# Looked-up ids broadcast by DMA as 16-bit halves, and empty GpSimd instructions between early gathers, in a recommendation tower on one core

## The reference, cut to what matters

```
e = stack([tbl_f[ids[:, f]] for f in 39 fields], axis=1)     # (512, 39, 32) float32
z = einsum('bpc,apc,bpa->bp', e[:, ROW], w, e[:, COL])       # 741 pairs (i<j) of fields
h = relu(concat([z, dense_ctx], 1) @ W_top1 + b_top1)        # 757 -> 512
h = relu(h @ W_top2 + b_top2)                                # 512 -> 256
y = h @ W_top3                                               # (512, 1)
```

## Time and profile before

| | |
|---|---|
| median of 3 runs | 199.92 us (199.55 to 202.13) |
| the profiled execution: its time | 198.71 us |
| its span | 197.0 us |
| granted TensorE clock | 1.00 of full |
| busy: TensorE, VectorE, GpSimd, ScalarE | 184.5, 144.1, 135.4, 42.7 us |

### The profile page before, as it was taken

One profiled execution on the slowest core, in us unless ns is written; L12 is line 12 of the kernel. 1 busy time (PEld: TensorE's weight loads), 2 busy tenths in 40 slices (PEclk: granted clock), 3 DMA queues, 4 the chain that ended last, 5 costly groups with the idle time before them and its releaser, 6 DMA issues.

```text
span 197.0 us, 3278 instructions
## 1 busy us (share of the span) xinstructions
PE 184.5 (94%) x1320; PEld 64.4 (33%) x1320; DVE 144.1 (73%) x137; ACT 42.7 (22%) x64; POOL 135.4 (69%) x202
## 2 busy tenths in 40 slices
PE   6999988969999999999999999799989976999895
PEld 3534533332222222322322222223322212222782
DVE  4889998965899989976663999589664349747600
ACT  4956941030001100111112100110121111210722
POOL 7988899888888888888888888888922200440000
PEclk9999999999999999999999999999999999999999
DMA  6999940000000100000000000000000000000000
GB/s 166 278 290 419 387 138 15 10 17 12 10 13 10 20 10 12 12 14 13 10 13 14 11 13 10 15 13 15 12 0 3 0 0 0 0 5 0 0 0 0
DMA packets 6688, 9.75 MB, mean 49 GB/s; under 512 B 1977, under 2 KB 4477, under 8 KB 6673
## 3 DMA queue, kind: packets, MB, share of 16 engines
q1 hardware_dynamic: 3696, 8.00, 12.6%
q0 software_dynamic: 2944, 1.51, 4.4%
q10 hardware_dynamic: 32, 0.03, 0.1%
HBM read 9.53 MB, written 0.00 MB: 48 GB/s over the span
## 4 chain that ended last, share of the span: by engine, by line
POOL 55%; PE 32%; issue 7%; DVE 2%; DMA 1%; ACT 1%; DVEq 0%; POOLq 0%
POOL gathered L395 41%; POOL pause L402 13%; PE ps L609 10%; PE ps L623 10%; PE ps L634 6%; PE ps L654 4%; PE ps L646 2%; DVE prod L518 2%; DMA gathered<-tbl,ids_sb 1%; POOL sel L384 1%; PE ps L587 1%; PE ps L663 0%; ACT eT L448 0%; POOL sel L387 0%; ACT z_sb L455 0%
## 5 line engine op out<-in xcount | busy, mean ns | idle before, releaser
L518 DVE TENSOR_TENSOR prod<-ps,eT 128x1024 f32<-128x1024 f32 (+2 forms) x91 | 110.2, 1265 | 36.2 <-PE ps L609 31.6
L395 POOL DMA_INDIRECT gathered<-tbl,ids_sb x92 | 92.3, 1003 | 15.2 <-issue 15.0
L609 PE MATMUL ps<-eT,w_sb 32*128 32x512 f32 (+2 forms) x380 | 70.7, 640 | 4.4 <-DVE prod L518 2.9
L623 PE MATMUL ps<-prod,sel 128*32 128x512 f32 x380 | 51.5, 604 | 0.0
L609 PEld LDWEIGHTS ps<-eT,w_sb 32*128 32x128 f32 (+2 forms) x380 | 22.0, 183 | 52.0 <-issue 25.1
L402 POOL MEMSET pause<- 128x256 f32 x91 | 30.3, 333 | 0.1
L503 DVE TENSOR_SCALAR hot<-ids_half,row_of 125x2048 bf16<-125x2048 f16 x34 | 27.8, 881 | 1.5 <-PE ps L576 0.9
L409 POOL TENSOR_TENSOR tabs<-tabs 128x512 f32<-128x512 f32 x8 | 10.1, 1264 | 25.0 <-ACT tabs L469 25.0
L576 PE MATMUL ps<-hot,lower 125*32 125x512 bf16 x272 | 22.0, 401 | 0.0
L634 PE MATMUL ps<-z_sb,w_sb 128*128 128x512 f32 x40 | 20.4, 624 | 0.7 <-ACT eT L448 0.7
L623 PEld LDWEIGHTS ps<-prod,sel 128*32 128x32 f32 x380 | 8.1, 108 | 33.7 <-issue 21.0
(11 more groups left out here) (36 smaller groups left out, 63.5 us busy)
## 6 DMA issues: line engine op xcount, KB each, us to landing
w_sb<-w SPq DMA_DIRECT2D x1, 1536.0 KB
gathered<-tbl,ids_sb POOLq DMA_INDIRECT x92, 2.3
tabs<-hot SPq DMA_DIRECT2D x3, 448.0 KB
w_sb<-wst SPq DMA_DIRECT2D x1, 640.0 KB, 13.1
w_sb<-wst SPq DMA_DIRECT2D x1, 576.0 KB, 12.0
tabs<-hot SPq DMA_DIRECT2D x1, 560.0 KB
w_sb<-wst SPq DMA_DIRECT2D x1, 512.0 KB, 10.5
w_sb<-w SPq DMA_DIRECT2D x1, 512.0 KB
```

The costliest lines, as they stand in the source:

```text
L395: pool.indirect_dma_start(gathered[J][:, b, K * r:K * r + K], None, tables[f], bass.IndirectOffsetOnAxis(ap=ids_sb[:, F * b + f:F * b + f ...
L518: dve.tensor_tensor(prod[:, x:x + n, :], ps[:, s:s + n, :], eT[:, I:I + 1, :].broadcast_to([P, n, B]), ALU.mult).then_inc(multiplied, 1)
L609: mm = pe.matmul(ps[:, RUN_BANK[p] + i - first, :], w_sb[rows, w_tile(q), :], eT[rows, J, :], start=True, stop=True)
L623: mm = pe.matmul(z_ps[K * (u % G):K * (u % G) + K, :], sel[:, u // G, :], prod[:, RUN_SLOT[p] + t - FIRST_TILE[p], :], start=(u < G), stop ...
```

## The change

The ids of the looked-up fields are laid out as 16-bit halves (the low half of each id) in one row of 2,048 for each h. Four loads, each of one such row to 125 partitions, take the place of the load, the conversion, the spreading matmuls and the copies. The load for h = 0 is on ScalarE's queue, the other three on SyncE's, each ahead of table h. `ids_half` is uint16 where it was float16. The "lower" step of h = 0 is cut into two halves of four slices, and "lower" 3 now stands behind "keep" 1 and before "keep" 2 on ScalarE. Look-up 2 has PSUM banks of its own (4, 5). Fourteen bf16 matmuls of 128 x 512 on zeros stand ahead of TensorE's work.

On GpSimd only the row numbers are made before the gathers. The five steps that make `ident` and `sel` follow gathers 1 to 5, one each. Between gathers 6 to 20 and their successors stand two `engine_nop`, each followed by a wait for its own semaphore. From gather 21 on there is the clear of `pause` as before.

```diff
-WARM = [2, 2]
+BARE = 20
+WARM = 14
+LOWER_PIECES = [[(0, 4), (4, 8)], [(0, 8)], [(0, 8)], [(0, 10)]]
...
-    steps += [("ids", 0), ("lower", 0), ("ids", 1), ("hot", 0, 0, 8), ("look", 0, 0, 3), ("lower", 1), ("ids", 2),
-              ("look", 0, 3, 8), ("keep", 0), ("lower", 2), ("ids", 3), ("hot", 1, 0, 8), ("look", 1, 0, 8),
-              ("lower", 3), ("keep", 1), ("hot", 2, 0, 8), ("look", 2, 0, 8), ("keep", 2), ("hot", 3, 0, 4),
+    steps += [("lower", 0), ("hot", 0, 0, 8), ("look", 0, 0, 8), ("lower", 1), ("keep", 0), ("hot", 1, 0, 8),
+              ("look", 1, 0, 8), ("lower", 2), ("keep", 1), ("hot", 2, 0, 8), ("look", 2, 0, 8), ("lower", 3),
+              ("keep", 2), ("hot", 3, 0, 4),
...
-        ids_half = [sb(f"ids_half{h}", [P, G, B], F16) for h in range(NHOT)]
+        ids_half = [sb(f"ids_half{h}", [P, G, B], U16) for h in range(NHOT)]
...
+            def load_hot_ids(h):
+                sp.dma_start(ids_half[h][0:HP, :, :].rearrange("p f b -> p (f b)"),
+                             hot_ids[h:h + 1, :].broadcast_to([HP, G * B])).then_inc(hot_ids_in[h], 16)
+
             sp.dma_start(ids_sb[:, :], ids).then_inc(ids_in, 16)
             load_table(0)
+            load_hot_ids(1)
             load_table(1)
+            load_hot_ids(2)
             load_table(2)
+            load_hot_ids(3)
...
+                    gathers += 1
+                    if gathers == 1:
+                        pool.memset(ident[:, :], 0.0).then_inc(consts_zero, 1)
+                    elif gathers == 2:
+                        pool.wait_ge(consts_zero, 1)
+                        pool.affine_select(out=ident[:, :], in_=ident[:, :], compare_op=ALU.not_equal, fill=1.0,
...
+                    elif gathers <= BARE:
+                        for _ in range(2):
+                            pool.engine_nop().then_inc(passed, 1)
+                            passes += 1
+                            pool.wait_ge(passed, passes)
+                    elif gathers < NCHUNK * len(fields):
+                        if pauses:
+                            pool.wait_ge(paused, pauses)
                         pool.memset(pause[:, :], 0.0).then_inc(paused, 1)
...
-            act.dma_start(hot_ids_sb[:, :], hot_ids).then_inc(hot_ids_in, 16)
-            act.wait_ge(hot_ids_in, 16)
-            act.activation(ids16[:, :], hot_ids_sb[:, :], ACT.Copy).then_inc(ids16_made, 1)
+            act.dma_start(ids_half[0][0:HP, :, :].rearrange("p f b -> p (f b)"),
+                          hot_ids[0:1, :].broadcast_to([HP, G * B])).then_inc(hot_ids_in[0], 16)
...
+            zeros = prod[:, 0, :].bitcast(BF16)
+            for _ in range(WARM):
+                pe.matmul(ps[:, 7, :], zeros[:, 0:P], zeros[:, 0:B], start=True, stop=True)
```

More of the change, by code:

```diff
@@ L207, in turns, with lowers_of @@
     return TURNS.index(J) + 1
-def halves_of(h):
-    return h + 2
+def lowers_of(h, c):
+    return 2 * (sum(len(pieces) for pieces in LOWER_PIECES[:h]) + 1 + [a <= c < b for a, b in LOWER_PIECES[h]].index(True))
 def lay_out_weights(w, W_top1):
@@ L246, in dlrm_tower @@
         row_of = {n: sb(f"row_of{n}", [P, n]) for n in ROW_SETS}
-        hot_ids_sb = sb("hot_ids_sb", [NHOT * G, B], I32)
-        ids16 = sb("ids16", [NHOT * G, B], F16)
-        spread = sb("spread", [NHOT * G, NHOT * G, HP], F16)
-        ids_half = [sb(f"ids_half{h}", [P, G, B], F16) for h in range(NHOT)]
+        ids_half = [sb(f"ids_half{h}", [P, G, B], U16) for h in range(NHOT)]
         tabs = sb("tabs", [P, G * K * sum(NSLICE)])
@@ L276, in dlrm_tower @@
         z_ps, side_ps = ps[:, 6, :], ps[:, 7, :]
-        look_ps = [[ps[:, bank, :] for bank in banks] for banks in [(0, 1), (2, 3), (0, 1), (6, 7)]]
-        ids_ps = [ps[0:HP, bank:bank + G, :] for bank in (0, 4, 4, 4)]
+        look_ps = [[ps[:, bank, :] for bank in banks] for banks in [(0, 1), (2, 3), (4, 5), (6, 7)]]
         h1_ps = [[ps[:, bank, of] for bank in banks] for of, banks in zip(HALVES, [(1, 5, 2, 3), (0, 4, 7, 6)])]
@@ L286, in dlrm_tower @@
         ids_in = sem("ids_in")
-        hot_ids_in = sem("hot_ids_in")
+        hot_ids_in = [sem(f"hot_ids_in{h}") for h in range(NHOT)]
         tab_in = [sem(f"tab_in{h}") for h in range(NHOT)]
@@ L306, in dlrm_tower @@
         paused = sem("paused")
+        passed = sem("passed")
         turned = sem("turned")
@@ L375, in _ @@
         def _(pool):
[L376 to L379, removed]
             for n in ROW_SETS:
                 pool.iota(row_int[n][:, :], pattern=[[1, n]], base=0, channel_multiplier=n).then_inc(rows_numbered, 1)
[L382 to L388, removed]
             pool.wait_ge(ids_in, 16)
             fields = [(J, r) for J in GATHERED for r in range(FIELDS_IN[J])]
-            pauses = 0
+            gathers = pauses = passes = 0
             for J, r in fields:
@@ L398, in _ @@
                     ).then_inc(rows_in[J], 16)
-                    if pauses:
-                        pool.wait_ge(paused, pauses)
-                    if (J, r, b) != (*fields[-1], NCHUNK - 1):
+                    gathers += 1
[4 more added lines that the diff above has]
+                        pool.affine_select(out=ident[:, :], in_=ident[:, :], compare_op=ALU.not_equal, fill=1.0,
+                                           base=0, pattern=[[-1, P]], channel_multiplier=1).then_inc(consts_made, 1)
+                    elif gathers == 3:
+                        pool.memset(sel[:, :, :], 1.0).then_inc(consts_zero, 1)
+                    elif gathers == 4:
+                        pool.wait_ge(consts_zero, 2)
+                        pool.affine_select(out=sel[:, :, :], in_=sel[:, :, :], compare_op=ALU.is_ge, fill=0.0, base=0,
+                                           pattern=[[P, ZM], [-K, K]], channel_multiplier=1).then_inc(consts_made, 1)
+                    elif gathers == 5:
+                        pool.wait_ge(consts_made, 2)
+                        pool.affine_select(out=sel[:, :, :], in_=sel[:, :, :], compare_op=ALU.is_ge, fill=0.0,
+                                           base=K - 1, pattern=[[-P, ZM], [K, K]],
+                                           channel_multiplier=-1).then_inc(consts_made, 1)
+                    elif gathers <= BARE:
[6 more added lines that the diff above has]
+                            pool.wait_ge(paused, pauses)
                         pool.memset(pause[:, :], 0.0).then_inc(paused, 1)
@@ L420, in _ @@
             for step in PLAN:
[L421 to L431, removed]
+                if step[0] == "lower":
                     h = step[1]
                     act.wait_ge(tab_in[h], 16 * len(tab_pieces))
-                    for i in range(2):
-                        act.activation(lower[i][h][0:HP, :, :], bytes_of[h][0:HP, :, 1 - i::4], ACT.Copy,
-                                       scale=256.0 if i == 0 else 1.0).then_inc(lower_made, 1)
+                    for a, b in LOWER_PIECES[h]:
+                        for i in range(2):
+                            act.activation(lower[i][h][0:HP, :, K * a:K * b],
+                                           bytes_of[h][0:HP, :, 4 * K * a + 1 - i:4 * K * b:4], ACT.Copy,
+                                           scale=256.0 if i == 0 else 1.0).then_inc(lower_made, 1)
                 elif step[0] == "keep":
@@ L461, in _ @@
                         act.wait_ge(mlp_in, 16 * len(mlp_loads))
-                        act.wait_ge(lower_made, 2 * NHOT)
+                        act.wait_ge(lower_made, lowers_of(NHOT - 1, NSLICE[-1] - 1))
                         act.wait_ge(hot_used, len(hot_block))
@@ L483, in _ @@
         def _(dve):
[L484 to L487, removed]
+            dve.memset(prod[:, 0, :], 0.0).then_inc(warm_zeroed, 1)
             n = K * FIELDS_IN[NBLK - 1]
             dve.memset(eT[n:P, NBLK - 1, :], 0.0).then_inc(pad_zeroed, 1)
-            dve.wait_ge(ids_spread, 3)
-            dve.tensor_copy(ids_half[0][0:HP, 2, :], ids_ps[0][:, 2, :]).then_inc(third_made, 1)
             for step in PLAN:
@@ L496, in _ @@
                         dve.wait_ge(rows_made, len(ROW_SETS))
-                        dve.wait_ge(ids_half_made, halves_of(h))
-                        dve.wait_ge(third_made, 1)
+                        dve.wait_ge(hot_ids_in[h], 16)
                     for c in range(c0, c1):
@@ L536, in side_free @@
                     pe.wait_ge(*side_used.pop())
[L538 to L541, removed]
             pe.wait_ge(warm_zeroed, 1)
-            keep_warm(2, WARM[0])
-            pe.wait_ge(ids16_made, 1)
-            pe.wait_ge(spread_made, 1)
+            zeros = prod[:, 0, :].bitcast(BF16)
+            for _ in range(WARM):
+                pe.matmul(ps[:, 7, :], zeros[:, 0:P], zeros[:, 0:B], start=True, stop=True)
             for step in PLAN:
[L548 to L559, removed]
+                if step[0] == "look":
                     h, c0, c1 = step[1:]
@@ L562, in _ @@
                         pe.wait_ge(tab_in[h], 16 * len(tab_pieces))
```

(8 more changed lines are left out.)

7 lines of the change are left out of this document (removed).

## The result

The changed kernel takes 207.74 us (median of 4 runs, 206.85 to 209.56); the kernel before took 199.85 us beside it (4 runs, 199.55 to 202.13). The ratio is 1.0381, with a 95% interval of 1.0275 to 1.0487: slower. The forecast was 197.7 us. The profiled execution took 207.24 us, with a span of 205.5 us, 8.5 longer than before.

What follows compares the result with a forecast made beforehand. Bound: TensorE's transpose of block 8, waiting for gather 80, with TensorE's own work behind. The smaller of 1.34 + 0.84 (X) = 2.2 and Y = 2.8 us gave 199.92 - 2.2 = 197.7 us; range 194.9 to 203.5 us.

Steps and rivals of the forecast that it cites:

- Where time is decided: TensorE's transpose of block 8 at 125.77 us, after 1.34 us idle; the end moves with it.
- The two times at block 8: When TensorE would be ready for that transpose (124.43 us) and when gather 80 has landed (125.73 us).
- the old wait of 1.34: TensorE's idle time in us before the transpose of block 8 in the kernel before.
- Y: How much earlier the gathers on GpSimd get: 3.1 saved by empty instructions less 0.3 for moved constants, 2.8 us.
- Five engines: Each 125-row ids load runs on five DMA engines, not 16, 25 rows on each; forecast with full pace 45%.
- X: How much earlier TensorE gets, decided before quad 0: 30.24 to 29.4 us, 0.84 us.
- table 3 comes late: Rival, 18%: slower DMA lands table 3 after 25.3 us, delaying quad 0 equally; 202.0 us halfway, 208.4 at 17.4 KB per us.
- The start of the tiles: VectorE's first one-hot tile, after ids h = 0 land behind 177 KB per engine: 9.7 us against 6.32.
- The premise that VectorE sets the pace of the opening: Before quad 0 TensorE follows VectorE's one-hot tiles; 24 tiles at 0.72 us, last slice done at 27.7 instead of 28.72.
- uint16: Rival, 5%: this type is slower on VectorE, 2.3 us a one-hot tile, 38 us more over 24 tiles.
- gathers in step with VectorE: Rival, 13%: opening gathers just miss the second one-hot tile, so intervals are three tiles, 2.1 us; 201.6 us.

Runs made afterwards that it cites:

- e5: Changed kernel with each ids load split into 112 and 13 partitions, run on another chip than the low-clock one: 199.56 us.
- e1: Changed kernel with each ids load split into 112 and 13 partitions, on a chip with a low clock for every kernel: 261.9 us.
- e2: Changed kernel with each ids load going to all 128 partitions in one piece, on the low-clock chip: 260.44 us.
- e11: Kernel before, with only the clears between gathers 6 to 20 replaced by two empty instructions each: 199.25 us, ratio 0.9970 to the kernel before.
- e9: Changed kernel with ids loads split, ident and sel made before the gathers, empty instructions between gathers 1 to 20: 196.68 us, ratio 0.9853 to the kernel before.
- e10: Changed kernel with ids loads split, ident and sel made before the gathers, empty instructions for every clear: 196.18 us, ratio 0.9849 to the kernel before.
- e8: Changed kernel with ids loads split and empty instructions between all gathers from 6 on, no clear at all: 196.22 us.

## Why the prediction was wrong

*Where time is decided: right.* The two times at block 8 account for the result: TensorE is ready at 134.27 us against 124.43, 9.8 later, gather 80 is long there, and the difference less the old wait of 1.34 is the span's 8.5.

*Y, GpSimd: right at gather 21, too large at gather 80, without effect on this result.* Gather 21 was predicted at 34.7 us and came at 34.83; Y at that gather is 2.7 us, against 2.8. The interval in the opening is (34.83 - 13.66)/15 = 1.41 us, taken as 1.45. Gather 1 began at 5.27, outside 3.2 to 4.5: the ids landed 4.2 us after their issue, beside the load of ids h = 0. The steps after it took less than summed, and gather 6 was off by 0.8 (13.66 against 12.9), so the good hit at gather 21 is in part errors that cancel. But block 8 waits for gather 80, and there Y is 1.8 us (121.41 against 123.17): the last one-hot tiles were made after 41 us here, beside gathers and clears that took up to 1.30 and 0.81 us instead of 0.95 and 0.33. In e5 Y at gather 80 is 1.3 us (121.91), and there it sets the time.

*Five engines: right.* SyncE's queue shows 4,086 packets, which is 3,336 + 375 rows + 375 completions, and those are 360 + 3 x 5. ScalarE's has 130, 125 rows and 5. The rule of the Trainium skill cited for it ("DMA: Bandwidth & Descriptors", section "Why a DMA increments its semaphore by 16 and not by 1") is what both queues show; e1, e2 and e5 show what it costs.

*X, the pace of the five engines: the step that failed.* "22.5 us at 25.7 KB per us, landed at 25.3": the same 578 KB landed at 34.9, in 32.1 us, so 18.0 KB per us. The mechanism and the bytes were right, the pace was not. I took it from the stretch of 14 to 22 us in the earlier trace rows. By the order of the queue that stretch carries weights and no table: the loads up to table 3 are 2.65 MB, and from 2 to 14 us 3.3 MB had been moved. The row of 2 to 8 us, with the tables' own rows of 4.1 KB, gave 17.4, and the window between the two, which the earlier trace rows leaves out, 267/16 = 16.7 KB per us. The kernel before:

```profile
8.00:14.00 6.00, 6.00 (x47) 2.03 (x49) 5.91 (x7) 3.85 (x5) 5.51 (x7) 1.00 1.06 267
```

At 17.4 throughout the rival "table 3 comes late" gives 208.4 us, against 207.74 measured; it stood at 18% and its far end outside the range, whose upper end of 203.5 has no working of its own. That it comes so near is partly luck: it has quad 0 at 40.1 us, which began at 38.73, and no term for the 1.4 us of low clock. The low pace is not one of five engines alone. In the changed kernel itself an engine moved 16.5 KB in each busy microsecond from 8 to 14 us (182/(16 x 0.69)). And in e5, with the ids on all 16, windows in the stretch in which tables and ids come show 247 to 264 GB/s at a DMA share of 1.05 to 1.06, which is 15.4 to 16.5 KB per us for each engine:

```profile
9.00:15.00 6.00, 5.98 (x112) 3.44 (x116) 6.00 (x9) 3.53 (x5) 5.51 (x6) 1.00 1.05 264
15.00:21.00 6.00, 6.00 (x120) 3.41 (x112) 6.00 (x9) 4.18 (x6) 4.73 (x6) 1.00 1.06 247
```

The start of the tiles shows little of the error, since only 177 KB lie before it: it was predicted at 9.7 and seen at 10.95, 1.25 us late, while table 3, behind 578 KB, is 9.6 late. The Trainium skill gives about 27 GiB/s for an engine ("DMA: Bandwidth & Descriptors", section "Specifications"). That is 29 KB per us, above every pace measured here, and would have made the step worse; the measurement decides.

*The premise that VectorE sets the pace of the opening: wrong, without effect on this result.* e11 took the clears out and freed 2.1 us of VectorE's time, and X stayed 0. In the kernel before and in e11, TensorE is busy 20.00 of the 20 us from 5 to 25 us, so it sets that pace, with the ids' spreading matmuls among its work.

*What was missing: a term for the clock.* The sum had nothing for TensorE's clock after a wait; the long wait ended at the lower level, and that cost 1.4 us. The rest follows: quad 0 predicted at 29.4, seen at 38.73, +9.3; with the clock +10.7; the forecast had the transpose of block 8 at 125.77 - 2.2 = 123.57, and it came at 134.27, 10.7 later.

*Other steps.* uint16 is as fast as float16 on VectorE: 6.41/9 = 0.71 us a tile in the changed kernel, against 0.85 in the earlier trace rows with clears beside it, and 9.45/14 = 0.68 for float16 in e11 without them. The rival "gathers in step with VectorE" did not come: the mean interval of 1.41 us is that of two tiles, not three.

## What to carry to other kernels

Before adding a load, count on how many engines it will run and sum up, engine by engine, all bytes up to the last transfer that somebody waits for, at the slowest pace that a row shows for rows of that size; the first arrival says little of the last. A partition count like 125 puts a large load on five of sixteen engines and delays everything queued behind it, here a table by 12 us, and splitting it into 112 and 13 mends this. When a bottleneck is removed, look which of the two streams is next: the split alone came level with before, and it won 3 us only when the gathers came sooner too, with the constants ahead of them again or with an empty pair in place of every clear.

## What was not expected of the hardware

- After short idle times TensorE's granted clock fell in some kernels and not in others. After the matmuls on zeros, e9 and e10 waited 2.82 and 2.69 us and ran their first look-ups at the lower level, 1.2 GHz; e5 waited 1.82 us and e8 3.29, and both ran them at 2.4. With it quad 0 began at 29.50 and 28.05 us in e9 and e10, against 26.36 in e5. At 162.7 us, e11 and e10 differ in the same way. Why it fell in one kernel and not in another is open. The windows of e9, with 0.50 of the clock up to 15 us, against 1.00 from 9 us on in e5 above:

```profile
9.00:12.00 3.00, 2.71 (x28) 1.27 (x32) 2.26 (x4) 1.47 (x4) 2.26 (x3) 0.50 1.05 278
12.00:15.00 3.00, 3.00 (x36) 1.28 (x28) 1.91 (x3) 1.77 (x2) 2.26 (x3) 0.50 1.03 254
```

- The load of the gathers' ids took 2.2 us from issue to landing before and 4.2 in the changed kernel, beside a load of 500 KB on the other queue where one of 32 KB had been; e10 and e5 show the same (gather 1 at 5.51 and 5.56). Whether that load is the cause was not tested.
- SyncE's queue itself was held: its first three weight loads took 1.30 us to issue before and 7.56 in the changed kernel. The timeline of it, before and changed:

```profile
3.83 1.30 SPq L348 DMA_DIRECT2D w_sb<-wst  x3
```

```profile
6.68 7.56 SPq L341 DMA_DIRECT2D w_sb<-wst  x3
```

- A pair of empty instructions with their waits between two gathers gives an interval of 1.31 us in the stretch of the quads (e8: 113.90 - 36.52 over 59), where the clear gave 1.45.
- Left open: why rows of 4.1 KB move at 15 to 18 KB per us for each engine; the kernel before had 16.7 to 17.4 without the broadcast rows, so these alone are not the reason. Whether e10 is really faster than e9 or e8 is not settled either.
